# Node 1/sqrt of four blocks at a time by Newton steps on VectorE, a rearranged end of binning, and scalar outputs by SiLU with gates as tanh plus one

## The reference

```python
h = jnp.maximum(_layernorm(x, axis=-1), 0.0)      # v - mean over 160 features, / sqrt(var + 1e-5)
skip_s = s @ W_skip0                               # s, v are the parts of h
skip_v = jnp.einsum('nmi,mk->nki', v, W_skip1)
s = s @ W_nl0
v = jnp.einsum('nmi,mk->nki', v, W_nl1)
rhat = edge_attr / jnp.linalg.norm(edge_attr, axis=-1, keepdims=True)
w = jax.nn.relu(edge_feature @ W_fc1) @ W_fc2
...                                                # tp: products of w, s[dst], v[dst], rhat
agg = jax.ops.segment_sum(tp, src, num_segments=N) / DENOM          # DENOM = 32
out_s = agg_s @ W_out_s + skip_s                   # 96 columns: 64 scalars, 32 gates
out_v = jnp.einsum('nmi,mk->nki', agg_v, W_out_v) + skip_v
fs = jax.nn.silu(out_s[:, :64])
gate = jax.nn.sigmoid(out_s[:, 64:96])
gv = gate[:, :, None] * out_v
x = x + jnp.concatenate([fs, gv.reshape(N, -1)], axis=-1)
```

## Time and profile before

| | us |
|---|---|
| median of 3 runs | 1369.47 |
| lowest, highest | 1368.71, 1371.86 |
| the profiled execution | 1372.43 |
| its span, first to last instruction | 1370.6 |
| DVE busy | 1214.9 (89%) |
| PE busy | 1213.3 (89%) |
| ACT busy | 1004.9 (73%) |
| POOL busy | 983.2 (72%) |

### The profile page before, as it was taken

The page is one execution under the profiler, slowest core; times in us unless marked ns, Lnnn a source line. Parts: engine busy times, 40 slices in busy tenths (PEclk is TensorE's granted clock), DMA queues, the critical chain, the costliest instruction groups (busy, mean ns, idle before and its releaser), DMA issues.

```text
span 1370.6 us, 33958 instructions
## 1 busy us (share of the span) xinstructions
PE 1213.3 (89%) x8857; PEld 995.2 (73%) x8857; DVE 1214.9 (89%) x4487; ACT 1004.9 (73%) x2379; POOL 983.2 (72%) x1135
## 2 busy tenths in 40 slices
PE   4999968999999999986888888888888888888886
PEld 2455537888888888875777777777777777777775
DVE  7999967888889888766999999999999999999996
ACT  3999966788888888855777777767677777767774
POOL 4333347788778888517888888888888888888883
PEclk9999988999999999998999999999999999999998
DMA  3000002344443444325787878778787778878774
GB/s 108 1 0 0 0 20 63 106 112 111 108 112 109 113 109 110 98 69 135 221 238 224 230 229 228 227 226 242 213 240 223 234 225 229 232 224 239 225 230 131
DMA packets 90920, 212.27 MB, mean 155 GB/s; under 512 B 15030, under 2 KB 56281, under 8 KB 90878
## 3 DMA queue, kind: packets, MB, share of 16 engines
q1 hardware_dynamic: 62462, 155.23, 35.9%
q0 software_dynamic: 28416, 56.56, 18.3%
HBM read 127.73 MB, written 84.00 MB: 154 GB/s over the span
## 4 chain that ended last, share of the span: by engine, by line
POOL 42%; PE 29%; issue 17%; DVE 7%; ACT 2%; DMA 1%; DVEq 1%; POOLq 0%; ACTq 0%; SPq 0%
POOL mg L565 32%; POOL n_rstd L571 8%; PE bank L1161 5%; PE bank L1098 4%; PE bank L1214 3%; PE bank L1190 3%; PE bank L1178 3%; PE bank L1145 2%; PE bank L1174 2%; PE bank L1176 2%; DVE rank_junk L717 2%; PE bank L1198 2%; ACT hn L962 2%; DVE bin_hot L681 1%; PE bank L1218 1%
## 5 line engine op out<-in xcount | busy, mean ns | idle before, releaser
L565 POOL DMA_INDIRECT mg<-messages,slot_m x392 | 453.6, 1157 | 121.1 <-issue 110.0
L1035 ACT ACTIVATE nn<-xb,n_bias,n_rstd 128x160 f32<-128x160 f32 x588 | 299.5, 650 | 111.3 <-DVE n_bias L662 109.8
L1240 PE MATMUL bank<-wsk_a,nt_a 128*128 128x160 f32 x1568 | 298.4, 313 | 55.0 <-DVE ob L845 53.2
L1240 PEld LDWEIGHTS bank<-wsk_a,nt_a 128*128 128x128 f32 x1568 | 226.7, 192 | 75.9 <-issue 52.0
L498 POOL DMA_INDIRECT xg<-x,dst_g x200 | 208.2, 1041 | 62.3 <-issue 57.1
L1042 ACT ACTIVATE nt_a<-bank 128x512 f32<-128x512 f32 x196 | 117.0, 597 | 105.8 <-PE bank L1233 105.8
L1254 PE MATMUL bank<-mg,hot 64*128 64x192 f32 x1568 | 181.2, 350 | 11.7 <-DVE hot L832 11.7
L644 DVE BATCH_NORM_STATS2 n_stat<-xb 128x6 f32<-128x160 f32 x784 | 186.7, 312 | 3.7 <-DMA xb<-x 3.4
L1232 PE MATMUL bank<-ident,nn 128*128 128x128 f32 x784 | 147.5, 311 | 35.2 <-ACT nn L1035 30.0
L1232 PEld LDWEIGHTS bank<-ident,nn 128*128 128x128 f32 x784 | 110.2, 210 | 91.6 <-issue 54.0
L571 POOL TENSOR_TENSOR n_rstd<-n_sum,neg_half 128x8 f32<-128x8 f32 x98 | 163.7, 1670 | 12.7 <-DVE n_sum L658 10.6
(11 more groups left out here) (172 smaller groups left out, 2724.4 us busy)
## 6 DMA issues: line engine op xcount, KB each, us to landing
xb<-x SPq DMA_DIRECT2D x97, 640.0 KB, 5.9
out_dram<-ob SPq DMA_DIRECT2D x97, 640.0 KB, 3.5
messages<-msg SPq DMA_DIRECT2D x50, 390.6 KB
mg<-messages,slot_m POOLq DMA_INDIRECT x392
ef<-edge_feat_t SPq DMA_DIRECT2D x50, 125.0 KB, 5.9
xg<-x,dst_g POOLq DMA_INDIRECT x200
xb<-x SPq DMA_DIRECT2D x1, 420.0 KB
out_dram<-ob SPq DMA_DIRECT2D x1, 420.0 KB
```

The costliest lines, as they stand in the source:

```text
L565: pool.indirect_dma_start(mg[:, u, k, :], None, messages[:, :], bass.IndirectOffsetOnAxis(ap=slot_m[:, u, k:k + 1], axis=0)).then_inc(n.g[ ...
L1035: last = act.activation(nn[:, u % 2, h, :, g % 4], xb[:, u, g, :], ACT.Relu, bias=n_bias[:, u, g:g + 1], scale=n_rstd[:, u, g:g + 1])
L1240: pe.matmul(z[:, t, 0:F], nt_a[:, h, t * P:(t + 1) * P], wsk_a[:], start=(t % 2 == 0), stop=False, skip_group_check=True)
```

## The change

Nothing of what is computed changes but the formulas in three places.

**Nodes.** GpSimd's power is gone. VectorE takes statistics for four macros at a time: `stats_n` runs 32 BN_STATS in pieces of 10, 11 and 11, in three of four rounds; in the fourth round (`extract`, i%4 = 2) it forms the 128x32 variances and their inverse roots. These are an integer shift (`halve`), a subtraction from a constant (`seed`), and three Newton steps of three operations each (`root_a`, `root_b`, `root_c`), every one of which waits for the one before by the semaphore `root`; then `shift_n`. The buffers of x grow from 4 to 8 (`XU`), SP loads macro i+7 in round i (seven loads at the start instead of three), and the hardware loop spans eight macros. `hot_n` makes the four one-hots with two TENSOR_TENSOR instead of four TENSOR_SCALAR. ScalarE takes the tanh of half the gate columns (`sg` now has 32 columns per node) and writes the SiLU of the 64 scalar columns straight into `ob`; VectorE adds one to the tanh in place and multiplies the 96 vector columns. The factor 1/2 goes into the weights. At the seam from the edges, VectorE takes the first 32 statistics in the rounds NG and NG+1 and the roots in NG+2; ScalarE's opening moves from NG+1 to NG+2.

**Binning.** Of each five tiles GpSimd now makes the last one's `slot_v` itself, by one TENSOR_SCALAR over 125x128 after its seven small operations; ScalarE makes the other four. **Its end.** The closing matmuls of zeros are gone (the last regular matmuls carry `stop`). VectorE computes `hat` and scales the weights right after its last tile, then reads the counts and the table out of PSUM and frees TensorE by `b_free`; the rest of `slots_i` and the overflow count (`table`) come in the first edge round.

```diff
-        U = 4
+        U, XU = 4, 8
+        AHEAD = (10, 21)
...
+                        pool.tensor_scalar(slot_v[:, r, :], iota_slot[0:ET, :], slot[:, k:k + 1], row_no[:, r:r + 1],
+                                           ALU.is_equal, ALU.mult).then_inc(b_last, 1)
...
-                    def ln_n(i, u):
-                        pool.wait_ge(n.var, i + 1)
-                        pool.tensor_tensor(n_rstd[:, u, :], n_sum[:, u, 4, :], neg_half[:, :], ALU.pow).then_inc(n.pw, 1)
...
                 edge_tiles(dve, tile_b)
-                dve.wait_ge(b_end, 1)
...
+                dve.wait_ge(s_sqrt, 1)
+
+                link(dve.reciprocal(vec_r[:], vec_r[:]))
...
+                dve.wait_ge(b_tab, NT)
+                dve.tensor_scalar(whole[:], p_cnt[(NT - 1) % 2], 1.0 / W_EVEN, None, ALU.mult).then_inc(b_free, 1)
                 dve.wait_ge(b_rows_sb, 1)
...
+                    dve.scalar_tensor_tensor(out=empty[:, r, :], in0=p_tab[r], scalar=0.0, in1=empty[:, r, :],
+                                             op0=ALU.is_gt, op1=ALU.mult).then_inc(b_free, 1)
...
+                    if isinstance(q, int) and q == 0:
+                        table()
                     if isinstance(q, int) and q == NG:
+                        nodes(main, False, (FIRST,))
...
+                    def root_a(i, u, k):
+                        b, base = u // U, level(i, u) + 3 * k
+                        y = n_rstd[:, b, :]
+                        dve.wait_ge(n.root, base + 7)
+                        dve.tensor_tensor(n_step[:, b, 0, :], y, y, ALU.mult).then_inc(n.root, 1)
...
+                        dve.scalar_tensor_tensor(out=n_step[:, b, 1, :], in0=n_step[:, b, 0, :], scalar=-0.5,
+                                                 in1=n_sum[:, b, 4, :], op0=ALU.mult, op1=ALU.mult).then_inc(n.root, 1)
...
+                        dve.scalar_tensor_tensor(out=y, in0=n_step[:, b, 1, :], scalar=1.5, in1=y,
+                                                 op0=ALU.add, op1=ALU.mult).then_inc(n.root, 1)
...
-                        dve.tensor_tensor(o[:, :, 0:S], z[:, :, 0:S], sg[:, h, :, 0:S], ALU.mult)
+                        dve.tensor_scalar(sg[:, h, :, :], sg[:, h, :, :], 1.0, None, ALU.add).then_inc(n.one, 1)
+                        dve.wait_ge(n.fs, 2 * i + h + 1)
+                        dve.wait_ge(n.one, 2 * i + h + 1)
...
-                        act.activation(sg[:, h, :, :], q_z[h][:, :, 0:SG], ACT.Sigmoid).then_inc(n.sg, 1)
+                        act.activation(sg[:, h, :, :], q_z[h][:, :, S:SG], ACT.Tanh, scale=0.5).then_inc(n.sg, 1)
+                        act.activation(ob[:, u % U, 4 * h:4 * h + 4, 0:S], q_z[h][:, :, 0:S], ACT.Silu).then_inc(n.fs, 1)
...
-                pe.wait_ge(b_fin, 1)
+                pe.wait_ge(b_free, 3)
                 pe.wait_ge(s_w, 16 * len(weight_loads))
```

More of the change, by code:

```diff
@@ L279, in __init__ @@
                 self.st = [sem(f"{name}_st{u}") for u in range(U)]
-        OPEN, ROUNDS = "open", "rounds"
+        FIRST, SECOND, OPEN, ROUNDS = "first", "second", "open", "rounds"
         main = Nodes("n")
@@ L418, in round_e, with nodes @@
                         store_msgs(q - 3, 1 - b % 2)
-                def nodes(n, every, parts=(OPEN, ROUNDS)):
+                def nodes(n, every, parts=(FIRST, SECOND, OPEN, ROUNDS)):
                     def load_x(i, u):
@@ L594, in _ @@
                 pool.wait_ge(e_st[1], 16 * (NG // 2))
[L595 removed]
+                nodes(main, False)
                 pool.wait_ge(b_fin, 1)
@@ L639, in _, with layer_norm @@
                 link(dve.tensor_scalar(weight[:], odd[:], W_ODD - W_EVEN, W_EVEN, ALU.mult, ALU.add))
-                def layer_norm(rows, stat, sums, chain, base, done, meanwhile=(None, None)):
+                def layer_norm(rows, stat, sums, chain, base, done):
                     for t in range(rows.shape[1]):
@@ new lines, in _ @@
+                dve.tensor_scalar(wo_u[V:2 * V, :], wo_u[V:2 * V, :], 1.5 ** 0.5 / 64.0, None, ALU.mult)
+                for j in range(2):
+                    same, cross = slice(2 * V * j, 2 * V * j + V), slice(2 * V * j + V, 2 * V * j + 2 * V)
+                    dve.tensor_scalar(wo_v[same, :], wo_v[same, :], 1.0 / 64.0, None, ALU.mult)
+                    last = dve.tensor_scalar(wo_v[cross, :], wo_v[cross, :], 1.5 ** 0.5 / 64.0, None, ALU.mult)
+                dve.tensor_scalar(wsk_a[:, SG:F], wsk_a[:, SG:F], 0.5, None, ALU.mult)
@@ L892, in nodes @@
                     if not every:
-                        hot_n(0, 0)
+                        hot_n(0, 0, 0)
+                        hot_n(0, 0, 1)
                     def round_n(i, u):
+                        before, after = (u + 7) % XU, (u + 1) % XU
+                        j, w = i + 2, (u + 2) % XU
+                        extract = u % U == 2 and macro_exists(j)
                         if macro_exists(i - 1):
-                            gate(i - 1, (u + 3) % U, 1)
+                            gate(i - 1, before, 1)
@@ L898, in round_n @@
+                        if extract:
+                            spread(j, w)
                         if macro_exists(i + 1):
-                            shift_n(i + 1, (u + 1) % U)
-                            norm_last(i + 1, (u + 1) % U)
+                            norm_last(i + 1, after)
+                        if extract:
+                            squares(j, w)
                         if macro_exists(i - 1):
-                            residual(i - 1, (u + 3) % U)
+                            residual(i - 1, before)
@@ L1253, in add @@
                             pair = 2 * h + t % 2
-                            last = pe.matmul(q_z[h][:, t, 0:Z], hot[slots, u % 2, pair, :], mg[slots, u, pair, 0:Z],
+                            last = pe.matmul(q_z[h][:, t, 0:Z], hot[slots, u % 2, pair, :], mg[slots, u % U, pair, 0:Z],
                                              start=False, stop=True, skip_group_check=True)
```

397 lines of the change are left out of this document (239 added, 158 removed).

## The result

The changed kernel takes 1306.6 us (median of four, 1305.0 to 1307.3) against 1369.2 us, 62.6 us less. The ratio is put at 0.952 with a 95% interval of 0.951 to 0.954; the two medians divided give 0.954. The profiled execution of after took 1305.0 us, its span is 1303.2 against 1370.6, 67.4 less. It stands 1.6 under its median, the one of before stood 3.2 above, so 4.8 of the 67.4 belong to the two executions.

A forecast was written before the change was run, and what follows sets the result against it. It took VectorE as the bound in binning, and VectorE and GpSimd together in the node stage. Nodes -68, end of binning -9.3 and disturbance +3 gave -74, so 1295.5 us against 1369.47; range 1282 to 1326.

The forecast's parts named there:

- The mechanism: Node stage: VectorE and GpSimd hand the round to each other, both need relief; round from 7.48 to 6.78 us.
- waits on others: Node stage: 0.08 us per round allowed for uneven VectorE rounds that do not fit TensorE's chain, making 6.78.
- the gate: Node stage, VectorE: addition 0.24 plus product 0.46 make 0.70 us in place of 0.79; two save 0.18.
- Roots: Node stage, VectorE: 18 operations on 32 columns once in four rounds take 3.06 us, between 1.6 and 5.4.
- Rival C: Node stage: dependent VectorE operations cost more than assumed, in roots and one-hots; round 7.07, 1324 us; chance 0.10.
- Rival A: Node stage: the loop of TensorE and ScalarE becomes the bound; round 6.92, 1309 us; chance 0.17.
- Rival D: Node stage: ScalarE switches function tables at every change between tanh and SiLU; +315, about 1679 us; chance 0.02.
- End of binning: After VectorE's last rank: weights and PSUM reads move into idle time, so the edge stage starts 9.3 us earlier.
- The disturbance: Binning: GpSimd's 40 new slot operations slow VectorE by 3 us, between 0 and 16.
- rival B: Binning: GpSimd's 40 new operations hold VectorE each time, 16 us in place of 3; 1308 us; chance 0.08.
- Start and seam: Kernel start and passage from edges to nodes: extra x loads hide, opening statistics and last message cancel; 0 us.
- nodes: Node stage as a whole: 97 rounds at 6.78 in place of 7.48 us save 68 us.

The follow-up runs named there:

- the fused gates: Changed kernel with each half's addition of one and product replaced by three scalar_tensor_tensor operations of 128 columns: 1268.2 us (ratio 0.925).
- the moved wait: Changed kernel with VectorE waiting for ScalarE's SiLU ahead of the addition of one, not between addition and product: 1295.8 us (ratio 0.946).
- useless power: Changed kernel plus one power over 8 columns of constants on GpSimd each round, which nothing waits for: 1349.4 us (ratio 0.984).
- the batched power: Changed kernel with VectorE's 11 seed and Newton operations replaced by one GpSimd power over 32 columns every four rounds: 1383.0 us (ratio 1.009).
- the table loads: Changed kernel with sigmoid for tanh beside SiLU, without the addition of one and halved weights; four table loads per round: 1670.2 us.

## Why the prediction was right, and where its sizes were off

**The mechanism** was right at both ends. VectorE's list sets the new round: it waits 1.9 us in 400, and four different edits (the wait, the fused gates, the old gates, two Newton steps) that took 0.12, 0.40, 0.07 and 0.18 us per round off the operations that they touched shortened the full rounds by 0.11, 0.40, 0.16 and 0.22. What the last two have beyond that lies in normalisations that came out shorter (0.06 and 0.05) and in the roots (0.03). GpSimd had to be relieved too: giving it 1.67 us back makes the round 7.36. That SP loads x seven macros ahead was not tested alone; VectorE had waited 1.9 us for x from 800 to 1200 us before, and doesn't now.

**The ledger.** Over 92 rounds (639.07 to 1278.07) all VectorE rows, from start to start, give 6.95 per round; the last rounds have no statistics left, which makes the mean 6.91. In us per round, forecast against measured:

| term | forecast | after |
|---|---|---|
| two additions | 0.48 | 0.71 |
| two products | 0.92 | 0.98 |
| two normalisations | 0.55 | 0.61 |
| residual | 1.40 | 1.40 |
| one-hots | 0.67 | 0.67 |
| statistics (0.239 and 0.228 each) | 1.91 | 1.78 |
| roots | 0.77 | 0.80 |
| waits on others | 0.08 | in the rows above (0.05) |
| sum | 6.78 | 6.95 |

The step that was mis-sized is **the gate**: 0.24 + 0.46 forecast, 0.354 + 0.491 measured, 0.29 per round, with 0.05 of it real waiting that I had as 0.08 elsewhere. I took the 0.03 of the earlier trace rows for the wait; the product has two waits in front and costs 0.11, which the moved wait shows to be 0.07 too much. And the addition, a TENSOR_SCALAR, lasts from 0.20 to 0.40, 0.24 in the mean. The forecast let the gates save 0.18 per round; they cost. Everything else agreed to 0.13, of which 0.04 is that the last of the 92 rounds hold no statistics.

**Roots**: 3.06 us forecast for 18 operations, 3.20 measured, Newton operations 0.22 apart as said. Rival C had the right suspicion, a dependent operation that costs more than rows 5 show, but put it on the roots, where it wasn't. **Rival A** gave 1309 us, nearer to the measured time than my forecast, by a mechanism that the runs refute: VectorE hardly waits in the changed kernel, and 6.92 was no floor, since the round went to 6.70 with two Newton steps and the gates untouched, and to 6.54 with fused gates. That 6.91 was measured is a coincidence. **Rival D** is refuted for tanh and SiLU (three loads in all) and confirmed in price for sigmoid and SiLU. The Trainium skill, "ScalarE: Activation LUTs", section "Table sets: the hidden batching unit", says to batch by set; the run with sigmoid agrees. The same page of the Trainium skill, section "What ACT_TABLE_LOAD costs", gives about 2.7 us a switch, drain included; here a load takes 1.28 us and the next activation starts 0.01 us behind it. The changed kernel's own rows show that tanh and SiLU share a set, which the table there doesn't list.

**End of binning**: forecast -9.3 and +3. Measured from the last rank to the first products: 27.15 us before, 17.73 after (188.16 to 215.31, 188.87 to 206.60), so -9.4. The disturbance is 0.7, not 3. The GpSimd operation lasts 0.81 us where I took 0.41, so 40 of them run for 33 us, and VectorE still lost under 1: **rival B** is refuted. The 0.703 of the earlier trace rows was weak ground for it: it is one of 50, the other 49 last at most 0.285, and it began at 217.75 beside GpSimd's power (L505, 217.26 to 218.31), with the first `cr_a` (L552, from 218.29) only at its end. The Trainium skill, "SBUF — State Buffer", section "Who interferes with whom", would allow either engine to be blocked; here it was hardly VectorE, whose rank reads PSUM; its one-hot of the bin lasts up to 486 ns now, 394 before.

**Start and seam**: forecast 0. The first products' lead of 8.7 grew to 11.1 by the seventh group and to 12.0 at the first residual. I had let the later groups run at the same pace, but the pipeline fills faster as well (2.4 us). Some 1.7 of that is luck with the clock, not the change. From the first products to those of the seventh group it takes 49.4 us before, where TensorE's clock is at the lower level for 3.4 us from 246.6, and 47.0 in the changed kernel, where it isn't; four runs with the same edge stage as the changed kernel that had such a stretch near 235 (one wait moved, useless power, two Newton steps, opening in one piece) took 48.7 to 48.8. The cause of the other 0.6 wasn't tested. That the opening cancels is right for the sum, but only because the change spreads it; in one piece it is some 9 us worse. From the last groups to the first residual the changed kernel is 0.9 faster.

**The sum**, against the profiles: nodes -55.4 for -68, the rest -12.0 for -6.3: -67.4 for -74. The nodes fell short by 12.6, the start made up 5.7 of it (2.3 disturbance, 2.4 filling, 0.9 seam, 0.1 end of binning), and 4.8 is the scatter of the two profiled executions, of which I had counted 3. So part of the nearness of 1295.5 to 1306.6 is luck: two misses of opposite sign.

## What to carry to other kernels

Where one engine's list is the bound, count distances from start to start, with the waits written in front of each operation: a second wait before an operation that depends on the one ahead cost 0.07 us, 196 times. Before moving work to another function or engine, price the old form and the new one both from rows; an edit that puts a smaller operation in the place of a larger one was 16 us more here. When two engines share a round, test each side by loading it without relieving the other: the useless power told in one run what the ledger could only claim.

## What the runs showed of the hardware

- Durations of VectorE's TENSOR_SCALAR in the node stage scatter (the addition 0.20 to 0.40, the two normalisations over 128x160 0.69 to 0.92 for the pair), those of TENSOR_TENSOR do not in the changed kernel (one-hots 409 to 425 ns). In the changed kernel 41 of 182 additions last over 0.26, and each of the 41 overlaps a gather that GpSimd is issuing; of the other 141 99 do. Overlap alone doesn't decide it: with the old gates 1 of 93 pairs of normalisations lasted over 0.76 us beside the same kind of gathers, here 26 of 92 did. The Trainium skill, "SBUF — State Buffer", section "Who interferes with whom", has TENSOR_SCALAR in its two-port modes take the port pair shared with GpSimd and TENSOR_TENSOR stay clear of GpSimd's descriptor writing; the rows of the changed kernel agree. In the two runs with a power on GpSimd in the node stage it isn't quite so: 10 of 376 one-hots by TENSOR_TENSOR last 432 to 479 ns, each of them beginning within 0.11 us of the start of a gather or a power.
- GpSimd's power costs by the column: 1.05 us for 4, 1.67 for 8, 5.97 for 32 (medians), 0.15 to 0.18 us a column, where a VectorE Newton chain of 11 operations on the same 32 columns takes 2.3 us.
- TensorE's granted clock over 700 to 850 us, a mean between the levels of 1.2 and 2.4 GHz, was 1.00 where it was busy 140 to 149 us, 0.97 at 135.10 (the useless power), 0.94 at 132.59 (the batched power, with its waits of some 5 us) and 0.86 at 108.23 (the table loads). Busy time alone doesn't decide: before, it was 1.00 at 131.60 of 150.
- One stretch of 3.4 us at the lower level, which one execution has and another of the same code has not, is worth 1.3 to 1.4 us in binning and 1.6 to 1.7 in the first edge groups. A difference of that size between two traces needs the clock's row beside it.
